# Last rows of a decoder layer in an order of their own, the last row's products on VectorE, slot weights in the expert tiles

## What is computed

```python
x = x + attn(layernorm(x))          # 16 heads of 16, rotary, causal softmax, out projection
x = x + xattn(layernorm(x), k, skip, ctx, ctx)
#   kv = v[...,:,None,:] * ctx[...,None,:,:]  (8x8 products per group)
#   y  = causal convolution of kv with k + kv * skip;  out = sum_i y * ctx
x = x + ffn(layernorm(x))
#   router: softmax over 16 experts, the 4 best, weights renormalised
#   shared = silu(x @ g) * (x @ u) @ down * sigmoid(x @ vec)
#   sparse = sum over the 4 chosen experts of weight * (silu(x@g_e) * (x@u_e)) @ down_e
```

## Time and profile before

| | us |
|---|---|
| median of 3 runs (620.38 to 621.9) | 620.7 |
| the profiled execution, its own time | 621.63 |
| its span | 619.8 |
| PE busy | 586.6 (95%) |
| VectorE busy | 491.2 (79%) |
| ScalarE busy | 415.8 (67%) |
| GpSimd busy | 396.7 (64%) |

### The profile page before, as it was taken

One profiled execution on the slowest core, in us unless ns is written; L12 is line 12 of the kernel. 1 busy time (PEld: TensorE's weight loads), 2 busy tenths in 40 slices (PEclk: granted clock), 3 DMA queues, 4 the chain that ended last, 5 costly groups with the idle time before them and its releaser, 6 DMA issues.

```text
span 619.8 us, 18806 instructions
## 1 busy us (share of the span) xinstructions
PE 586.6 (95%) x5901; PEld 459.8 (74%) x5901; DVE 491.2 (79%) x1516; ACT 415.8 (67%) x1060; POOL 396.7 (64%) x439
## 2 busy tenths in 40 slices
PE   7899899999999999999999999978899999999991
PEld 3558679888888898898888988966476766767661
DVE  4548788989978989899878768577567789988983
ACT  3777977877868778778677586542266666666661
POOL 1237767879888878878788878596200356555554
PEclk9999999999999999999999999899899999999997
DMA  6935333244333143242302011002444677777753
GB/s 179 304 103 170 100 99 124 77 127 135 99 128 109 57 137 97 93 152 88 105 28 96 27 62 53 19 26 80 151 126 127 168 224 225 235 221 228 226 172 118
DMA packets 55682, 78.95 MB, mean 127 GB/s; under 512 B 7330, under 2 KB 46370, under 8 KB 55588
## 3 DMA queue, kind: packets, MB, share of 16 engines
q1 hardware_dynamic: 37300, 48.51, 25.8%
q0 software_dynamic: 6912, 18.88, 10.3%
q10 hardware_dynamic: 11376, 10.36, 4.8%
HBM read 44.43 MB, written 33.29 MB: 125 GB/s over the span
## 4 chain that ended last, share of the span: by engine, by line
PE 80%; POOL 6%; issue 6%; ACT 2%; DVE 2%; DMA 1%; SPq 1%; POOLq 0%; DVEq 0%; ACTq 0%
PE ps L774 11%; PE ps L656 9%; PE ps L553 7%; PE ps L586 6%; PE ps L487 5%; PE ps L678 5%; PE ps L786 4%; PE ps L797 4%; PE ps L541 4%; PE ps L606 4%; PE ps L590 3%; PE ps L763 3%; POOL kv_lo L1481 2%; PE ps L524 2%; PE ps L514 2%
## 5 line engine op out<-in xcount | busy, mean ns | idle before, releaser
L1481 POOL TENSOR_TENSOR kv_lo<-kv,kv_hi 128x512 f16<-128x512 f32 x64 | 80.3, 1256 | 30.5 <-ACT kv_hi L912 30.3
L1551 POOL DMA_INDIRECT toeplitz_lo<-y_slots,slots x44 | 42.8, 974 | 78.3 <-DMA y_slots<-kv 56.1
L774 PE MATMUL ps<-w_gate_up_hi,toeplitz_hi 128*128 x316 | 83.6, 313 | 0.4 <-DVE toeplitz_hi L1389 0.4
L1520 POOL DMA_INDIRECT x_slots<-x_norm,slots x64 | 69.1, 1080 | 18.9 <-issue 14.4
L1469 POOL TENSOR_TENSOR kv<-ctx_t_sb,v_t 128x512 f32<-128x512 f32 x64 | 69.1, 1089 | 15.9 <-ACT v_t L901 15.8
L881 ACT ACTIVATE probs<-ps,row_neg_max 128x128 f32<-128x128 f32 x256 | 71.6, 392 | 0.5 <-DVE row_neg_max L1086 0.3
L553 PEld LDWEIGHTS ps<-v_ones,probs_t 128*128 128x128 f32 x512 | 62.2, 192 | 2.2
L553 PE MATMUL ps<-v_ones,probs_t 128*128 128x17 f32 x512 | 60.7, 256 | 0.0
L586 PE MATMUL ps<-kv_hi,toeplitz_hi 128*128 128x128 f16 x256 | 56.6, 221 | 3.3 <-POOL kv_lo L1481 1.8
L995 ACT ACTIVATE toeplitz_hi<-ps 128x256 f16<-128x256 f32 x79 | 30.3, 383 | 43.5 <-ACT stage L1014 17.4
L586 PE MATMUL ps<-kv_lo,toeplitz_hi 128*128 128x128 f16 x256 | 56.3, 220 | 0.0
(11 more groups left out here) (226 smaller groups left out, 2079.1 us busy)
## 6 DMA issues: line engine op xcount, KB each, us to landing
stage<-in_w_units SPq DMA_DIRECT2D x36, 512.0 KB, 3.9
x_slots<-zeros SPq DMA_DIRECT2D x15, 512.0 KB, 4.8
toeplitz_hi<-x_slots SPq DMA_DIRECT2D x40, 128.0 KB
y_slots<-stage ACTq DMA_DIRECT2D x40, 128.0 KB, 3.7
y_slots<-kv ACTq DMA_DIRECT2D x39, 128.0 KB, 2.7
kv_hi<-x_slots SPq DMA_DIRECT2D x20, 128.0 KB
x_slots<-zeros SPq DMA_DIRECT2D x1, 2432.0 KB, 12.8
kv_lo<-x_slots SPq DMA_DIRECT2D x19, 128.0 KB, 2.6
```

The costliest lines, as they stand in the source:

```text
L774: last = nc.tensor.matmul(psum[2 + t % 2][:, 0:2 * INTER], bxT[a][t % 2][:, kc, :], egu[b][:, bass.ds(e, 1), kc, :].rearrange("p a n -> p ...
L1481: nc.gpsimd.tensor_tensor(flat(kvh[1][g % 2]), kv[g % 2][:].rearrange("p h j i -> p (h j i)"), flat(kvh[0][g % 2]), ALU.subtract).then_inc ...
L1520: pool.indirect_dma_start(out=xbuf, out_offset=bass.IndirectOffsetOnAxis(ap=slots[:, row, j:j + 1], axis=0), in_=xn[2][row % 2][:], in_off ...
L1551: pool.indirect_dma_start(out=yg[n][j], out_offset=None, in_=ybuf[0:(last_tile(row, j) + 1) * P], in_offset=bass.IndirectOffsetOnAxis(ap=s ...
```

## The change

- Steps 0 to 16 keep the strings of `ORDER`, without the weight pieces (`se ss sr cw c1 c3`, `c2`). The rest of the row stage (`DRAIN_FROM` = 17 on) is written out as four lists (`DRAIN`) of piece and row: PE, ACT, DVE and POOL each have their own. `order()` and `LAST_FIRST` are gone. The index shifts in `PREPARE_LO` only follow from the removed pieces.
- In the lists PE takes row 15's `t3` before `px:13` and `t4:14`, `ga0:13` behind `wo:15`, and mixes the pieces of rows 13, 14 and 15. `px:15` stands ahead of `dn:13`. The whole PE list is: px:12 ga1:12 v:15 sc01:15 up0:12 sc23:15 up1:12 pt0:15 cv0:14 Th0:12 pt1:15 at0:15 cv1:14 cv2:14 t5:13 pt2:15 Th1:12 at1:15 pt3:15 at2:15 at3:15 ro:13 t2:15 cv3:14 wo:15 ga0:13 dn:12 t3:15 px:13 t4:14 ga1:13 cv0:15 cv1:15 up0:13 cv2:15 t5:14 cv3:15 ro:14 up1:13 t4:15 px:14 Th0:13 Th1:13 ga0:14 up0:14 t5:15 ro:15 ga1:14 px:15 dn:13 up1:14 ga0:15 up0:15 Th0:14 Th1:14 ga1:15 up1:15 dn:14 Th0:15 Th1:15 dn:15. Before, the order from step 17 was that of each full step: px:12 ... ro:13 ga0:13 t2:15 cv3:14 wo:15 dn:12 t4:14 t3:15, then px:13 and so on.
- `LATE_BANKS` deals the banks anew for these pieces.
- Row 15's products `kv0..3` run on VectorE and read v from PSUM; for that `t3` writes v in the order in which `vT` used to leave it. Row 15's second residual goes to a buffer of its own (`x2_last`).
- `px` has one more product that puts `tile_end` into PSUM, and `pa` reads it there.
- The weights of the choices are made by `weigh` on VectorE in the tile stage, four rows at a time: 28 instructions, one in each of the tile steps 2 to 29. `slot_key` and `router_exp` are kept for all rows.
- Four products of zeros stand ahead of the tiles, not 16. SP issues the first eight tile loads before it stores row 15's `x_shared`. The second and third part of the table come after `dn:14` and `Th1:15`.

Row 15's store moved behind the first eight loads; row 14's is now the last store ahead of them. The diff, cut to its core:

```diff
+DRAIN_FROM = NB + 1
+DRAIN = {n: [(p.split(":")[0], int(p.split(":")[1])) for p in pieces.split()] for n, pieces in {
+    "PE": "px:12 ga1:12 v:15 sc01:15 up0:12 sc23:15 up1:12 pt0:15 cv0:14 Th0:12 pt1:15 at0:15 cv1:14 cv2:14 t5:13 "
+        "pt2:15 Th1:12 at1:15 pt3:15 at2:15 at3:15 ro:13 t2:15 cv3:14 wo:15 ga0:13 dn:12 t3:15 px:13 t4:14 ga1:13 "
...
+LATE_BANKS = (
+    "cv0:14 xT:13 o2T:14 cv0:15 xT:14 o2T:15 xT:15 up0:15",
+    "cv3:14 vT:15 cv3:15",
+    "cv2:14 cv2:15 ro:14 px:14 ro:15 px:15 up1:15",
+    "",
+    "wo:15 px:13 up1:13 ih1:13 up1:14 ih1:14 ih1:15",
+    "ih0:12 ro:13 up0:13 ih0:13 up0:14 ih0:14 ih0:15",
+    "cv1:14 ga0:13 cv1:15 ga0:14 ga0:15",
+    "pt2:15 ga1:13 ga1:14 ga1:15",
+)
...
-        key = ring("slot_key", 2, [P, EXPERTS])
+        key = sb("slot_key", [P, NB, EXPERTS])
+        causal_sb = key[:].rearrange("p b e -> p (b e)")[:, 0:P]
...
+        x2_last = st[:, 2752:2752 + E]
+
+        def x2_of(row):
+            return x2[row % 2][:] if row < NB - 1 else x2_last
...
+        def bank(use, row=0):
+            return psum[LATE_HOME.get((use, row), HOME[use][0])]
 
         def free(pe, use, row):
-
+            if (use, row) in LATE_AFTER:
+                u, r = LATE_AFTER[use, row]
+                READER[u][0].wait(pe, r, READER[u][1])
+                return
...
+                            and not (name == "store_shared" and row == NB - 1):
...
                 load_tile(t)
+            store_shared(NB - 1)
...
+                to = bank("vT")[:, 0:E].rearrange("p (h c i) -> p c h i", c=KC, i=SIDE)
...
+                    last = nc.tensor.matmul(to[:, c], xn[1][0][:, c * P:(c + 1) * P], id_sb[:].rearrange("p (h i) -> p h i", i=SIDE),
+                                            is_transpose=True, start=True, stop=True, skip_group_check=True)
...
+                nc.tensor.matmul(part(3, 4), share, many(tile_end[:], 1), start=True, stop=True, skip_group_check=True)
...
-            for s in range(NB + DEPTH):
+            for s in range(DRAIN_FROM):
                 if s == 1:
                     pe.wait_ge(s_once, 4)
                 for name, behind in ORDER["PE"]:
                     if 0 <= s - behind < NB:
                         pieces[name](s - behind)
-                    if s - behind == NB - 1 and name in table_after:
-                        table_after[name]()
                     if (s, name) in first_rows:
                         keep_busy(*first_rows[(s, name)])
+            for name, row in DRAIN["PE"]:
+                pieces[name](row)
+                if (name, row) in table_after:
+                    table_after[name, row]()
 
...
-            keep_busy(16, 7)
+            keep_busy(4, 7)
...
+                nc.scalar.activation(vT[row % 2][:].rearrange("p h i -> p (h i)"), bank("vT")[:, 0:E], ACT.Copy)\
...
+            def products_kv(g):
+                def piece(row):
+
+                    vT_ready.wait(dve, row)
+                    dve.wait_ge(s_c[row % 2], 16 * (row // 2 + 1))
+                    kv_ready.wait(dve, row - 1)
+                    if g < 2:
+                        kv_hi.wait(dve, row - 1, g + 3)
+                        kv_lo.wait(dve, row - 1, g + 3)
+                    else:
+                        kv_hi.wait(dve, row, g - 1)
+                        kv_lo.wait(dve, row, g - 1)
+                    part = slice(SIDE * g, SIDE * (g + 1))
+                    vs = bank("vT")[:, 0:E].rearrange("p (h a i) -> p h a i", a=1, i=SIDE)[:, part]
+                    cs = c_sb[row % 2][:, part].rearrange("p h (j a) -> p h j a", a=1)
+                    nc.vector.tensor_tensor(kv[g % 2][:], cs.broadcast_to([P, SIDE, SIDE, SIDE]),
+                                            vs.broadcast_to([P, SIDE, SIDE, SIDE]), ALU.mult).then_inc(kv_ready.sem, 1)
+                return piece
...
+                if row < NB - 1:
+                    xsh_ready.wait(dve, row - 2)
+                nc.vector.scalar_tensor_tensor(out=x2_of(row), in0=bank("o2T")[:, 0:E], scalar=1.0 / WS,
...
-            def select(row):
-                picked_done.wait(dve, row)
-                ex_done.wait(dve, row)
-                sel_step.wait(dve, row - 1)
-                nc.vector.scalar_tensor_tensor(out=esel[:], in0=picked[row % 2][:, 0:EXPERTS], scalar=-NEG,
-                                               in1=ex[row % 2][:], op0=ALU.is_equal, op1=ALU.mult)\
-                    .then_inc(sel_step.sem, 1)
-
...
-                nc.vector.tensor_tensor(ahead[:], newest[row % 2][:], tile_end[:], ALU.subtract).then_inc(page_step.sem, 1)
+                nc.vector.tensor_tensor(ahead[:], newest[row % 2][:], bank("px", row)[:, 3 * EXPERTS:4 * EXPERTS], ALU.subtract)\
+                    .then_inc(page_step.sem, 1)
...
-                hit_step.wait(dve, row - 2, 1)
-                nc.vector.scalar_tensor_tensor(out=key[row % 2][:], in0=picked[row % 2][:, 0:EXPERTS], scalar=-NEG,
+                nc.vector.scalar_tensor_tensor(out=key[:, row, :], in0=picked[row % 2][:, 0:EXPERTS], scalar=-NEG,
...
-            def find_slot(row):
-                k8_done.wait(dve, row)
-                hit_step.wait(dve, row - 1)
-                nc.vector.tensor_tensor(hit[:], key[row % 2][:].rearrange("p (a e) -> p a e", a=1)
-                                        .broadcast_to([P, TOP, EXPERTS]),
-                                        k8[row % 2][:, 0:TOP].rearrange("p (j a) -> p j a", a=1)
-                                        .broadcast_to([P, TOP, EXPERTS]), ALU.is_equal).then_inc(hit_step.sem, 1)
-
...
+            def weigh(n, k):
+
+                rows = slice(QUADS * n, QUADS * (n + 1))
...
+                if k == 0:
+                    nc.vector.tensor_scalar(wanted, slots[:, rows].rearrange("p b j -> p (b j)"), 1.0, None, ALU.add)\
+                        .then_inc(weigh_step.sem, 1)
+                elif k == 1:
+                    nc.vector.tensor_tensor(
+                        each, key[:, rows].rearrange("p b (j e) -> p b j e", j=1).broadcast_to([P, QUADS, TOP, EXPERTS]),
+                        wanted.rearrange("p (b j e) -> p b j e", b=QUADS, e=1).broadcast_to([P, QUADS, TOP, EXPERTS]),
+                        ALU.is_equal).then_inc(weigh_step.sem, 1)
+                elif k == 2:
+                    nc.vector.tensor_tensor(each, each, ex[:, rows].rearrange("p b (j e) -> p b j e", j=1)
+                                            .broadcast_to([P, QUADS, TOP, EXPERTS]), ALU.mult).then_inc(weigh_step.sem, 1)
+                elif k == 3:
+                    nc.vector.tensor_reduce(picked_ex, hit.rearrange("p (s e) -> p s e", e=EXPERTS), X, ALU.add)\
+                        .then_inc(weigh_step.sem, 1)
+                elif k == 4:
+                    nc.vector.tensor_reduce(ex_sum, of, X, ALU.add).then_inc(weigh_step.sem, 1)
+                elif k == 5:
+                    nc.vector.reciprocal(ex_recip, ex_sum).then_inc(weigh_step.sem, 1)
+                else:
+                    nc.vector.scalar_tensor_tensor(
+                        out=cw4[:, rows], in0=of, scalar=1.0 / WS, in1=ex_recip.rearrange("p (b j) -> p b j", j=1)
+                        .broadcast_to([P, QUADS, TOP]), op0=ALU.mult, op1=ALU.mult).then_inc(weigh_step.sem, 1)
...
+                weigh_step.wait(dve, row // QUADS)
...
+                if 0 <= s - 2 < 7 * QUADS:
+                    weigh(*divmod(s - 2, 7))
...
-            def weigh_slot(row):
-                hit_step.wait(pool, row, 1)
-                sel_step.wait(pool, row)
-                cw4_done.wait(pool, row - 2)
-                nc.gpsimd.tensor_tensor(hitw[row % 2][:], hit[:], cwe[row % 2][:].rearrange("p (a e) -> p a e", a=1)
-                                        .broadcast_to([P, TOP, EXPERTS]), ALU.mult).then_inc(hit_step.sem, 1)
```

143 lines of the change are left out of this document (61 added, 82 removed), and 36 rows, old and new, of tables (DRAIN, ORDER, PREPARE_LO).

## The result

| | before | after |
|---|---|---|
| median | 621.74 us (22 runs, 618.83 to 625.79) | 623.18 us (22 runs, 622.02 to 625.14) |
| the profiled execution | 621.63, span 619.8 | 623.25, span 621.4 |
| mean granted clock of it | 0.987 | 0.984 |

The ratio after to before is 1.0035, 95% interval 1.0023 to 1.0046: some 0.35% slower. I had predicted 617.4 us with 613.2 to 621.2. The sign was wrong.

The account below looks back on a forecast made before the run. PE was taken to bound the full steps and tiles, with room in the last rows. Zeros -2.8, waits -0.6, pa -0.8, px +0.5, weights +0.4, clock 0 gave -3.3: from a 620.7 median to 617.4 us, range 613.2 to 621.2.

Parts of the forecast that it names:

- Zeros, -2.8: Ahead of the tiles: cutting zero products from 16 to 4 saves 2.8 us, bounds 1.0 and 2.8.
- 0.9 to spare: First tile loads: 3.9 us from fin:14 to use fits in PE's 4.8 us after dn:14, leaving 0.9.
- Row 15's convolution: Last rows: kv on VectorE at 0.68 us each brings cv3:15 at 411.1 and not 416.3.
- the freed 0.8 of `pa`: Step 18: pa reading PSUM frees 0.8 us of VectorE ahead of r2, on which cv0:15's bank waits; counted as -0.8.
- The waits, 6.6 to 6.0: PE's waits in the last rows, from 380.99 on, fall from 6.6 to 6.0 us; saved 0.6, bounds 3.0 and 9.0.
- the walk's own 6.9: Last rows: carrying the four engine lists on with the old durations gave PE 6.9 us of waits; 6.0 was taken.
- The clock, saved 0: End of the row stage: again two low-clock stretches, 3.6 us, saved 0; one less or more is 1.8 either way.
- A third stretch, between `t4:15` and `px:15` where I have 3 us of waits: Rival, last rows: a third low-clock stretch there costs 1.8 us, giving 619.2; chance 0.06.
- `px` +0.5, weights +0.4: One more product per px costs 0.5 us in all; weights on VectorE in the tiles cost 0.4, bounds 0 and 8.4.
- The sum: Whole kernel: -2.8 zeros, -0.6 waits, -0.8 pa, +0.5 px, +0.4 weights, clock 0, together -3.3 us.
- The slower rival: Tile stage: VectorE becomes the bound through the weights' instructions, up to 625.4 us; chance 0.08.

Follow-up runs that it names:

- fill16: The changed kernel with 16 zero products ahead of the tiles instead of four: 626.16 us, ratio 1.0068 to the kernel before.
- old4: The changed kernel with the old order, old banks and row 15's products on GpSimd; four zeros and late row 15 store kept: 620.81 us, 0.9990 to before.
- fix_b: The changed kernel with only hl0:13 moved ahead of row 14's slots on VectorE: 622.98 us, ratio 1.0034 to the kernel before.
- weights_only: The changed kernel with old order, banks, 16 zeros, row 15's store ahead of the loads and its products on GpSimd: 621.44 us, 0.9992 to before.
- fix_abs: The changed kernel with hl0:13 ahead of row 14's slots, sct3:13 ahead of rt3:15, and row 14's store behind the first eight loads: 619.52 us, 0.9962 to before.
- again: The changed kernel measured once more without any edit: 623.05 us, ratio 1.0014 to the kernel before.
- store14: The changed kernel with only row 14's store moved behind the first eight loads: 624.04 us, ratio 1.0044 to the kernel before.
- fix_a: The changed kernel with only sct3:13 moved ahead of rt3:15 on GpSimd: 623.55 us, ratio 1.0047 to the kernel before.
- fix_ab: The changed kernel with hl0:13 moved ahead of row 14's slots and sct3:13 ahead of rt3:15, stores unchanged: 619.89 us, ratio 0.9979 to before.
- kv_pool: The changed kernel with hl0:13 and sct3:13 moved earlier, row 14's store behind the loads, and row 15's kv products back on GpSimd: 622.28 us, 1.0025 to before.
- fix_abs0: The changed kernel with hl0:13 and sct3:13 moved earlier, row 14's store behind the loads, and no zeros ahead of the tiles: 619.36 us, 0.9982 to before.
- fill_gap: The changed kernel with 13 zero products in PE's idle time, nine behind ga0:14 and four behind t5:15: 622.34 us, ratio 1.0033 to before.

## Why the prediction was wrong

**Zeros, -2.8.** Right in the new order: 2.8 in the profile, 3.1 by the median (`fill16`). In the old order (`old4`) it was 1.7 in the profile and nothing in the median. The loads were issued at 441.32, after `x_shared` of row 14 and its store, and only the second tile waited, 0.97 us. I had 0.9 to spare; it was about nothing.

```profile
437.46 3.76 SPq L428 DMA_DIRECT2D shared_sum<-x_shared  x2
441.32 2.06 SPq L484 DMA_DIRECT2D toeplitz_hi<-x_slots  x4
```

**Row 15's convolution.** `kv` on VectorE took what I had read off `gm`:

```profile
L1163 DVE TENSOR_TENSOR kv<-ctx_t_sb,ps x4: 682/685/689, 405.0 to 409.9; 128x512 f32<-128x512 f32 x4
```

`t3:15` stood 20.7 us behind `px:12` (I said 21.7), and `cv3:15` 31.0 behind it (30.0, at 411.1 against 381.09): 1.0 late, and 2 late beside `t3`. Part of that is `nm3:14`, released late (0.9 ahead of `t5:14`), the rest `x` of row 14 (0.9 ahead of `cv0:15`). I had priced the freed 0.8 of `pa` there, though my list of waits had none ahead of `cv0:15` that it could shorten. `pa` did fall to the time that the earlier trace rows have as its best, and the operation in front of it took over the place, 1.23 us where its median is 0.23:

```profile
406.40 1.23 DVE L1239 TENSOR_TENSOR_SCAN tile_newest<-ones_f,tile_newest,tile_opened 128x16 f32<-128x16 f32 x1
407.66 0.17 DVE L1244 TENSOR_TENSOR tile_ahead<-tile_newest,ps 128x16 f32<-128x16 f32 x1
```

GpSimd ran two `kl` from 406.43 on. So the 0.8 were not to be had: what waits for GpSimd there is the next small operation on SBUF operands, not `pa` as such. The Trainium skill's page SBUF — State Buffer ("SBUF: two separate sides") has VectorE's operation wait for the whole of GpSimd's; this row agrees, 1.23 us beside a `kl` of 1.16, and so does `tile_end` (1.19, median 0.17) beside the last `kl`. `slots` took 0.80 (median 0.27) and ended with a `kl` as well, with only one SBUF input.

**The waits, 6.6 to 6.0.** This is the step that failed: they were 8.3. I listed 0.5 ahead of `t2`, 0.4 at `cv2:15`, 1.75 and 0.9 ahead of `ro`, 1.8 ahead of `up0:14`, 0.3 and 1.2 ahead of `px:15` and `dn:15`. Measured at these places: 0.6, 0.3, 0.8 and 0.9, 2.4, 0 and 1.0, together 6.1, what my sum had for all of them. The 2.2 on top are three waits that I didn't have, 0.9 ahead of `cv0:15`, 0.9 ahead of `t5:14` and 0.4 ahead of `dn:14`. The first two lead back to VectorE's small operations beside the `kl`. The scan above stands ahead of `x` of row 14 and took 1.0 longer than its median. `nr3:14`, which releases `nm3:14`, stands behind `slots` and `tile_end`, which took 0.5 and 1.0 longer than theirs:

```profile
411.14 0.80 DVE L1278 TENSOR_SCALAR slots<-slot_top 128x4 int32<-128x4 f32 x1
412.05 1.19 DVE L1264 SCALAR_TENSOR_TENSOR tile_end<-tile_fresh,tile_end 128x16 f16<-128x16 f32 x1
413.16 0.20 DVE L1087 TENSOR_SCALAR ln_shift<-ln_mean_var,ln_rstd 128x1 f32<-128x1 f32 x1
```

I had cut the walk's own 6.9 to 6.0, since many small operations don't wait for GpSimd at full length; those next to the `kl` did. This is read from the rows; no experiment takes these waits out.

The two waits that the experiments take out are another matter. The one ahead of `up0:14` I had, at 1.8; it was 2.4. What I didn't have is its twin. My walk carried the order of each queue and the readers of the banks, but not that a buffer in SBUF is read by DMAs until they land. `sct3:13` behind `rt3:15` holds `nm3:15` 2.5 us, in parallel with `up0:14`; it is hidden in PE's list because PE waits there for something else already, and it shows as 2.4 ahead of `t5:15` as soon as the other is gone (`fix_b`). It added little to the miss. It is why the wait ahead of `up0:14` could not be removed alone.

**The clock, saved 0.** In the two profiles it looks right, and isn't. The loss by the clock's rows in the last rows is 3.3 us before (at 396 and 438) and 3.4 after, all of it now between 424 and 431. But the two stretches before come and go: `weights_only` and `old4`, with the same order there, have neither, and of the changed order's profiles only `fix_abs` has one near 400. The one from 424 on is in all five profiles that keep the wait ahead of `up0:14` with nothing in it (the changed kernel, `again`, `fill16`, `store14`, `fix_a`); `fix_b`, with the wait at `t5:15`, has half as much, from 426.1; and `fix_ab`, `fix_abs` and `kv_pool`, with both waits out, have none there. Over the executions on the first chip, (1 - clock) times the span has a median of 6.8 us before, 9.3 in `again` and 5.6 in `fix_abs`. So the change added low clock here, and taking the two waits out removed most of it; `fix_abs0` shows that some can stay. "A third stretch, between `t4:15` and `px:15` where I have 3 us of waits" was a rival at 0.06: the place was right, and I had written those waits down myself; the chance should have gone with them. First the row: in this stretch the granted clock fell to 0.50 after PE had idled 2.41 us; with the idle time filled (`fill_gap`) it stayed at 1.00. The Trainium skill's page TensorE: Matmul & The Clock Gate ("HAM oscillation — how this bites in real kernels") describes a kernel that loses the clock each time its TensorE waits for a transfer. Those waits are longer than the 2.41 us here, so the page alone does not foretell this loss; the trace decides, and here the clock was lost.

**`px` +0.5, weights +0.4.** Right. From row 0's `px` to row 12's the kernel before took 294.0 and the changed one 294.5. From tile 2 to the last tile it took 155.48 before, 155.27 in the changed kernel's profile, and 155.8 in the mean over the changed kernel and the twelve others: +0.3. VectorE is not the bound in the tiles.

**The sum.** Measured from the two profiled executions, +1.6 against my -3.3, 4.9 apart: 1.8 is the low clock near 58 us that the kernel before didn't have in its profile. Some 3.2 are in the last rows: from `px:12` to the first tile 61.3 us, where I had 62.3 less the 4.2 of zeros, waits and `pa`, 58.1. The waits (2.3 more than in the sum) and the 0.8 of `pa` make 3.1 of these 3.2. `fix_ab` took 57.8, `fix_abs` 59.0 with one low stretch near 400. That `fix_ab` comes so near my 58.1 is luck: it gets there without a wait that I had counted. Its waits are 6.9 us and it has no low clock in these rows, while I had 6.0 and 3.6 of low clock, taken from an execution that was 2.1 us longer by it than `weights_only`.

The two waits don't close the gap to the forecast either. My forecast is 0.995 of the 620.7 that I started from. Taking both waits out brings the median to 0.998 (`fix_ab`) or 0.996 (`fix_abs`) of the kernel before, from some 1.003. So 1 to 2 us stay that no experiment here assigns; some 1 us more is that the kernel before has a median of 621.74 over 22 executions, and not 620.7. (`fix_ab`'s profiled execution, 618.27, flatters it: it is 1.6 us under its own median.)

**The slower rival** was VectorE in the tiles, 0.08. The side was right and the place wrong.

**Open.** Row 0's `px` stood at 87.09 us in the kernel before, and in the changed kernel's family between 87.25 and 89.21, in eight of thirteen profiles behind 88.6. These eight are the ones with a low stretch ahead of it, near 59 us in three (the changed kernel, `weights_only`, `fill_gap`) and near 32 us in five; the other five and the kernel before have none, and their `px` stands between 87.1 and 88.2. `again`, near 32 us and near 58 us:

```profile
31.80:35.30 3.50, 3.44 (x12) 1.76 (x12) 1.35 (x2) 2.58 (x4) 0.00 (x0) 0.51 0.20 40
58.00:62.50 4.50, 3.69 (x48) 3.46 (x49) 2.94 (x6) 2.28 (x4) 2.89 (x4) 1.00 0.81 223
```

`fix_abs` (87.60) and `fix_abs0` (88.88) have the same instructions up to there, so it comes and goes. Whether the change makes it more frequent, one profile of the kernel before can't tell. It may hold a part of the 0.1 to 0.4%. Whether `fill_gap`'s 1.4 us of the profile are in its median is open too.

## What to carry to other kernels

A queue's order must be walked with all that frees a buffer, transfers that read it included: a DMA placed behind a waiting operation on its queue frees its source late, and the engine that wants that buffer may not be the one in the list of waits. Two waits that stand in parallel are worth nothing singly; look behind the longest one before moving it, and move both. Small VectorE operations on a chain, beside long GpSimd operations, are to be counted at the length of the GpSimd operation: here 1.23 for 0.23, 1.19 for 0.17 and 0.80 for 0.27 us. Where the walk leaves TensorE waiting twice within a few microseconds, price the low clock with it, but by its effect on the stretch's length: here it was some 1.4 us of the 3.6 that went with the two waits. And ask of a profile that a forecast starts from whether its low-clock stretches are in other executions too: here 2.1 us of the last rows were not.

## What was not expected of the hardware

The granted clock varies between executions of one program. Over 30 executions of the kernel before on the last chip, (1 - clock) times the span went from 3.7 to 8.7 us, and a microsecond of it went with 0.7 us of time (0.6 and 0.5 on the other two). Near 58 us the clock is 0.62 in some executions and 1.00 in others of nearly the same instructions. In the kernel before it fell near `dn:15` after waits of PE of 1.29 and 1.15 us; `weights_only`, with waits of 1.0 and 1.15 there, stayed at 1.00. A clock loss isn't time lost in full: in the changed kernel's stretch of 9.25 us it was 2.3 by the clock row, and 0.8 when it was taken away. That the rest was hidden behind ScalarE's and VectorE's part of the chain is likely, and not shown.
